# One f32 head product instead of two split ones for the last two batches' group norm, and attention's row maxima spread in two partition parts

## The reference, cut to what matters

```
# layer 0: cross attention to 375 context tokens, 16 heads of 32
a = layernorm(ctx) ; Q, K, V = x Wq, a Wk, a Wv
attn = softmax(Q K^T / sqrt(32)) ; x = x + tanh(gate) * (attn V) Wo
# layer 1: RWKV block, 32 heads of 16
xk, xw, xv, xr, xg = mixes of ln1(x) and its token shift
s = k v^T + w * s ; out = r (u * k v^T + s)            # over the 112 tokens
m  = out.mean(over the 16 of a head)
va = ((out - m) ** 2).mean(over the 16 of a head)
og = (out - m) / sqrt(va + 1e-5) * gn_w + gn_b          # group norm by head
x1 = x + (og * silu(xg Wg)) Wo
xc = ln2(x1) ; result = x1 + sigmoid(..xc.. Wfr) * (relu(..xc.. Wfk)^2 Wfv)
```

## Time and profile before

| | |
|---|---|
| median of 3 runs | 1399.43 us (1397.38 to 1405.21) |
| the profiled execution, its own time | 1399.84 us |
| its span from first to last instruction | 1398.0 us |
| mean granted TensorE clock | 0.979 |
| busy shares | PE 94%, DVE 67%, ACT 54%, POOL 38% |
| `least_cols` | 32 transfers of 437.5 KB |
| `ctx_tok` | 16 pairs of transfers, 672.0 KB (112 partitions) and 78.0 KB (13 partitions) |

### The profile page before, as it was taken

How to read it: one execution, slowest core, us unless ns; L and a number is a source line. 1 busy time by engine, 2 the same in 40 slices (tenths; PEclk the granted TensorE clock), 3 DMA queues, 4 the chain that set the end, 5 groups by cost and what they waited for, 6 DMA issues and landing times.

```text
span 1398.0 us, 42906 instructions
## 1 busy us (share of the span) xinstructions
PE 1319.0 (94%) x17120; PEld 936.5 (67%) x17120; DVE 939.5 (67%) x2416; ACT 752.2 (54%) x1804; POOL 528.5 (38%) x582
## 2 busy tenths in 40 slices
PE   6999999999999999897899999999999999999967
PEld 5777777777777777666666666766676666667624
DVE  3555555555555555547578888888888789887852
ACT  4776677676676677532434453445444544454342
POOL 2221112222222222113547545654566355644550
PEclk9999999999999999987899999999999999999978
DMA  7333322222222222213000010010100010000000
GB/s 228 100 105 107 98 63 69 75 71 70 65 76 76 76 69 92 63 50 136 15 14 22 22 28 14 23 27 21 24 14 26 21 28 11 25 21 21 8 15 14
DMA packets 39402, 73.48 MB, mean 53 GB/s; under 512 B 17781, under 2 KB 20469, under 8 KB 37701
## 3 DMA queue, kind: packets, MB, share of 16 engines
q1 hardware_dynamic: 39237, 71.01, 17.2%
HBM read 60.01 MB, written 7.57 MB: 48 GB/s over the span
## 4 chain that ended last, share of the span: by engine, by line
PE 73%; DVE 13%; issue 8%; ACT 2%; DMA 2%; POOL 1%; SPq 1%; DVEq 0%; POOLq 0%; ACTq 0%
PE b_bank L2017 15%; PE b_bank L2023 12%; PE ring_bank L703 7%; PE ring_bank L704 6%; PE ring_bank L705 6%; PE av_bank L789 4%; PE score_banks L762 4%; DVE probs L450 3%; PE b_bank L2132 3%; PE score_banks L749 3%; PE b_bank L2158 2%; DVE bv L1404 2%; DVE probsT L467 2%; PE av_bank L775 2%; DVE ktil L1398 1%
## 5 line engine op out<-in xcount | busy, mean ns | idle before, releaser
L1139 POOL TENSOR_TENSOR rst<-rp,st 128x448 f32<-128x448 f32 x192 | 202.5, 1078 | 34.9 <-DVE st L1425 32.0
L450 DVE CUSTOM_DVE_ANT_0 probs<-score_banks,unmask 112x375 f32<-112x375 f32 x256 | 124.9, 545 | 93.0 <-issue 93.0
L595 ACT ACTIVATE probs<-probs,least_inv 112x375 f32<-112x375 f32 x256 | 152.7, 609 | 32.5 <-DVE least_inv L450 32.5
L467 DVE SCALAR_TENSOR_TENSOR probsT<-score_banks,least_cols 125x448 f32<-125x448 f32 x192 | 108.0, 618 | 54.2 <-PE score_banks L762 51.8
L610 ACT ACTIVATE probsT<-probsT,key_mask 125x448 f32<-125x448 f32 x192 | 114.7, 662 | 47.6 <-DVE probsT L467 47.4
L1131 POOL TENSOR_TENSOR xm<-mixed,xa 128x448 f32<-128x448 f32 x80 | 89.6, 1129 | 96.1 <-DVE mixed L1354 90.7
L375 POOL TENSOR_TENSOR ctx_rstd<-ctx_var_eps,a_eps_exp 125x3 f32<-125x3 f32 x16 | 13.9, 866 | 272.7 <-DVE ctx_var_eps L423 272.7
L340 POOL TENSOR_TENSOR aT_lo<-whole,aT_hi 128x375 fp32r<-128x375 f32 x64 | 59.0, 922 | 152.3 <-ACT whole L576 150.2
L703 PE MATMUL ring_bank<-aT_hi,wk_lo 128*128 128x376 f32 x256 | 91.2, 356 | 0.9 <-issue 0.9
L1159 POOL TENSOR_TENSOR cen_r<-wkv,sq_r 128x448 fp32r<-128x448 f32 x15 | 17.1, 1140 | 196.6 <-ACT sq_r L1829 196.6
L1354 DVE SCALAR_TENSOR_TENSOR mixed<-b_bank,vec_sb,sx 128x112 f32<-128x112 f32 x320 | 82.5, 324 | 5.6 <-POOL xm L1131 3.9
(11 more groups left out here) (197 smaller groups left out, 3156.6 us busy)
## 6 DMA issues: line engine op xcount, KB each, us to landing
least_cols<-values_of_two_batches SPq DMA_DIRECT2D x32, 437.5 KB
ctx_tok<-in_ctx SPq DMA_DIRECT2D x16, 672.0 KB
xT_sb<-in_xT SPq DMA_DIRECT2D x16, 224.0 KB, 3.0
inv_cols<-values_of_two_batches SPq DMA_DIRECT2D x128, 28.0 KB, 3.7
x_tok<-in_x SPq DMA_DIRECT2D x16, 224.0 KB, 2.7
x_between_layers<-x_tok SPq DMA_DIRECT2D x16, 224.0 KB, 4.6
b_x<-x_between_layers SPq DMA_DIRECT2D x16, 224.0 KB, 2.6
out_dram<-ln_tok SPq DMA_DIRECT2D x16, 224.0 KB, 2.3
```

Source lines behind the costliest of these rows:

```text
L450: dve.tensor_tensor_reduce(out=probs[:, g % 2, i], in0=score_bank[0:T, i, 0:TC], in1=unmask[:, m[1]], scale=-SCALE, scalar=-LOWEST, op0=AL ...
L467: dve.scalar_tensor_tensor(out=probsT[:, g % 2, k].rearrange("p (i t) -> p i t", t=T), in0=score_bank[0:TK, :, k * T:(k + 1) * T], scalar= ...
L595: act.activation(probs[:, g % 2, i], probs[:, g % 2, i], ACT.Exp, scale=-1.0, bias=least_at(m, g, i), accum_out=sums[:, g, i:i + 1]).then_ ...
L1139: pool.tensor_tensor(by_chunk(rst[:, j % NPROD]), by_chunk(rp[:].rearrange("p c t -> p (c t)")), state_of(j), ALU.mult).then_inc(s_pprod, 1)
```

## The change

**Attention.** `spread_rows` reads the maxima back in two transfers, to partitions 0 to 111 and 112 to 124, in place of one to 125. The semaphore that DVE waits on now gets 32 instead of 16 per spread. This is done for all 16 batches.

**Group norm.** For batches 14 and 15 (`in_last_step`) the split is gone. `gn_centre` is one matmul call on `wkv` itself and `gn_var` one on the square, with the matrices read as f32. `norm_high`, `norm_low`, `square_high` and `square_low` are not called for these two batches. PE waits for `wkv_sum` directly and later for `square` directly; the waits that guarded the buffers moved to `square` and `gn_centre`. The 14 batches before keep the split.

```diff
-            sp.dma_start(least_cols[:, 2 * half:2 * half + 2],
-                         rows_in_dram(half, 0).rearrange("(o g) f -> o g f", o=1).broadcast_to([TK, 2, HG * T])).then_inc(s_least_in[half], 16)
+            for part in CTX_PARTS:
+                sp.dma_start(least_cols[part, 2 * half:2 * half + 2],
+                             rows_in_dram(half, 0).rearrange("(o g) f -> o g f", o=1).broadcast_to(
+                                 [part.stop - part.start, 2, HG * T])).then_inc(s_least_in[half], 16)
...
-                dve.wait_ge(s_least_in[g // 2], 16 * count(m, 1, 1))
+                dve.wait_ge(s_least_in[g // 2], 32 * count(m, 1, 1))
...
+    def in_last_step(l):
+
+        return isinstance(l[0], int) and index(l) >= B - 2
...
         def last_steps():                          # gpsimd
             rec_key(m)
-            norm_low(l)
-            square_low(l)
...
             rstd2(l)
-            norm_low(m)
-            square_low(m)
             gate_output(m, False)
...
         def square(l):                             # scalar
             act.wait_ge(s_cen, count(l, 1, 1))
             if is_last(l):
                 act.wait_ge(s_rmm, count(l, 1, 1))
+            elif in_last_step(l):
                 act.wait_ge(s_gated, count(later(l, -1), 1, 1))
...
-            pe.wait_ge(s_gnlo, count(l, 2, 1))     # gn_centre
+            pe.wait_ge(*((s_wkv, count(l, 1, 1)) if in_last_step(l) else (s_gnlo, count(l, 2, 1))))
             if is_last(l):
+                pe.wait_ge(s_gmm, count(l, 1, 1))
...
+            if in_last_step(l):
+                pe.matmul(norm_bank(l)[0][:, 0:CT], centring[:].bitcast(F32), wkv[:].rearrange("p c t -> p (c t)"), start=True,
+                          stop=True).then_inc(s_cen, 1)
+                return
...
-            pe.wait_ge(s_gnlo, count(l, 2, 2))     # gn_var
+            pe.wait_ge(*((s_sq, count(l, 1, 1)) if in_last_step(l) else (s_gnlo, count(l, 2, 2))))
...
+            if in_last_step(l):
+                pe.matmul(norm_bank(l)[1][:, 0:CT], mean_r[:].bitcast(F32), norm_home(l)[1].rearrange("p c t -> p (c t)"), start=True,
+                          stop=True).then_inc(s_var, 1)
+                return
```

More of the change, by code:

```diff
@@ L1152, in norm_low @@
             pool.wait_ge(s_gnhi, count(l, 2, 1))
-            if is_last(l):
-                pool.wait_ge(s_gmm, count(l, 1, 1))
-            elif at_least(l, 1):
+            if at_least(l, 1):
                 pool.wait_ge(s_gaff, count(later(l, -1), 1, 1))
@@ L1824, in norm_high @@
             act.wait_ge(s_wkv, count(l, 1, 1))
-            if is_last(l):
-                act.wait_ge(s_rmm, count(l, 1, 1))
-            elif at_least(l, 1):
+            if at_least(l, 1):
                 act.wait_ge(s_gated, count(later(l, -1), 1, 1))
@@ L1832, in square @@
             act.wait_ge(s_cen, count(l, 1, 1))
+            if is_last(l):
+                act.wait_ge(s_rmm, count(l, 1, 1))
+            elif in_last_step(l):
+                act.wait_ge(s_gated, count(later(l, -1), 1, 1))
             flat = "p c t -> p (c t)"
@@ L1879, in last_steps @@
             chunk_keys_decayed(m)
-            norm_high(l)
             copy_keys(m)
@@ L1886, in last_steps @@
             square(l)
-            square_high(l)
             gn_rstd(l)
             gn_affine(l)
-            norm_high(m)
             square(m)
-            square_high(m)
             xc_affine(l)
```

## The result

Over 14 runs each the changed kernel took 1394.60 us (median, 1390.20 to 1399.38) and the kernel before 1399.74 us (1395.47 to 1405.21): a ratio of 0.9964, 95% interval 0.9948 to 0.9980. That is 5.1 us; the interval leaves 1 out, and the size is under the 0.5% of the prediction's middle case. The predicted 1394.8 lies 0.2 us from the median; the interval allows a gain of 2.8 to 7.3 us, so that a hit this close is luck. The profiled execution took 1396.23 us (span 1394.4, mean clock 0.983), 3.6 us less than the profiled one of before.

A forecast was written before the change was run, and what follows sets the result against it. PE, busy 94% of the span, was taken as the bound, with DMA waits at the seam and waits and clock in the tail. Gains of 2.96 + 0.63 + 1.22 = 4.81 us gave 1394.8 us, 8-in-10 range 1390.8 to 1398.6.

The forecast's parts named there:

- middle case: Whole kernel: measured difference within about 0.5%, 7.0 us, of none; chance 0.75.
- The landing of `least_cols`: At the seam: two parts use more DMA engines and land 3.0 us after issue instead of 6.10.
- Rival 1: At the seam: the two parts land no sooner, 2.96 us not gained, 1398.4 us; chance 0.12.
- The seam, 2.96 us: DVE starts scores 1.47 us earlier, and PE's clock staying up behind the shorter idle time gives 1.49 us.
- both terms pass on: Behind the seam: all later work waits for this chain, so wait and clock gains pass on, 2.96 us.
- Batch 14's group norm, 0.63 us: Tail: PE no longer waits for POOL's second subtraction; DVE is late next, so normalisation, gate and `project_out` come 0.63 us earlier.
- Batch 15's, 1.22 us: Tail: ACT's cast and the split ahead of centring go, 1.83 us, less the f32 call's extra time at low clock.
- the other end: Batch 15's group norm with the clock up: gain of about 2.2 us.
- The sum: Whole kernel: 2.96 + 0.63 + 1.22 = 4.81 us gained, clock turns in the tail put at zero.
- Rival 2: Tail: the clock stays up under batch 14's `project_out`, 8.0 us gained in all, 1391.8 us; chance 0.17.
- Rival 3: Tail: low clock from batch 15's centring lasts through the dense products, 10.4 us lost, 1405.4 us; chance 0.04.
- Rival 4: Seam as forecast, but the tail's 1.85 us taken back by a low-clock `wfk` stretch, 1396.6 us; chance 0.17.

The follow-up runs named there:

- parts of 62 and 63: Changed kernel with the maxima spread in parts of 62 and 63 partitions instead of 112 and 13: 1399.75 us, ratio 1.0003 to the kernel before.
- one transfer of 128: Changed kernel with one maxima transfer over 128 partitions instead of two over 112 and 13: 1395.43 us, ratio 0.9975 to the kernel before.
- group norm alone: Kernel before with only the group norm edit (f32 head products of the last two batches, no splits): 1397.65 us, ratio 0.9993.
- attention part alone: Kernel before with only the attention edit (maxima spread in two parts): 1397.38 us, ratio 0.9989.
- tail filled: Changed kernel with 14 unread matmuls of 128 x 256 in front of TensorE's waits in the last step: 1390.31 us, ratio 0.9939.
- last spread only in parts: Changed kernel with two parts only in the very last maxima spread, the other 31 in one transfer: 1392.83 us, ratio 0.9951.
- fillers in both kernels: Unread matmuls at TensorE's long waits (seam, early steps, last step): kernel before 1389.22 us, changed kernel 1384.26 us.
- everything filled and f32 for all batches: Changed kernel with unread matmuls at TensorE's long waits and f32 head products in all 16 batches: 1377.80 us, ratio 0.9851.

## Why the prediction was right

**The landing of `least_cols`.** The reason (5 of 16 engines) was right, and parts of 62 and 63 and one of 128 show it. The share was 0.81 from 1 to 2 us behind the issue, near the 0.9 forecast. The landing of 3.0 us was too hopeful as far as is known: the transfer of 128 over 16 engines takes a median of 3.7 us, and it shares the queues with the four `inv_cols` behind it; for the two parts no row gives a landing. It cost nothing, since DVE comes 4.3 us after the issue and waits for nobody. Rival 1, a landing no sooner, is excluded.

**The seam, 2.96 us.** Measured 3.12: the wait 1.57, the clock 1.56. That 0.82 us of idle time would leave the clock up was right in every kernel with the faster landing (nine traces, idle time 0.82 to 0.90 us, S 14.78 to 14.87).

**That both terms pass on to the end** is not shown. At the first chunk sums the gain is still there (39.70 us from the third key-major scores before, 36.45 after), though the way from the `wk` product to them scatters: 20.3 to 21.8 us in the traces without fillers behind the seam. Further on it shrinks. From the third key-major scores to the chunk sums at the head of the loop, in traces without fillers in between:

| kernel | us |
|---|---|
| before | 178.00 |
| group norm alone | 178.50 |
| attention part alone | 175.43 |
| one transfer of 128 | 176.68 |
| tail filled | 177.48 |
| last spread only in parts | 177.72 |
| changed | 178.66 |

The last five have the whole gain of the seam and are on average 1.1 us faster than the first two, not 3.1; the best is 2.8 us faster, the changed kernel's own trace 0.4 us slower. Over the 140 us behind the first chunk sums the granted clock was 0.96 in the best of them and 0.91 in the changed kernel, where it was 0.94 in both of the slower landing; in the other three it was 0.94 as well, and what takes their part back is open. (With f32 products in all batches it is 174.99 us, but there these steps are changed too.) With fillers in both kernels the gain passes on: 173.32 us before and 171.55 with the change, for 1.36 of S. The medians can't tell whether 3.1 or 1.1 us arrive: the attention part alone gained 1.5 us, with an interval from 0.8 us slower to 3.9 us faster.

**Batch 14's group norm, 0.63 us.** Measured 0.59. The variance starts 4.45 instead of 6.11 us behind the chunk sums, 1.66 us sooner, and DVE, named as next late, takes all but 0.6 of it.

**Batch 15's, 1.22 us.** Measured 1.18 in the traces where the clock is low there, and 1.90 with fillers in both kernels, where I had put 1.83 + 0.12 plus faster transposes, about 2.2, as the other end. The f32 centring took 1.86 us at the low clock, 0.14 more than the bound of 1.72.

**The sum** of 4.81 us stands against 3.12 + 0.59 + 1.18 = 4.89 by the legs and 5.1 by medians. The three terms are measured each at its place, and to 0.2 us. That their sum is also the difference of the medians rests in part on luck: the interval leaves 2.2 us to either side, and the other legs, put at zero, were +1.22, +2.76, -1.25 and -1.37 us in the one profiled pair, each as large as a term of the sum. Rival 2 (clock up under `project_out(l)`) did not come true as a rule, but it occurs: that product took 3.69 us in two of the seven kernels with f32 products and an unfilled tail (group norm alone, one of 128) and 5.4 to 6.7 in the other five. Where it occurred, the way from the last chunk sums to the `wfk` of batch 15 is 47.06 us; 51.93 less the 1.77 of the two legs would be 50.16, so it is worth 3.1 us, and I had 3.2. In the profiled changed kernel (48.97) some 1.2 us of it are there. Whether the edit made it likelier is open. Rival 3 did not occur. Rival 4's `wfk` stretch did not get longer (4.95 us, and 4.89 before); its time of 1396.6 alone would lie inside the interval.

What I had not asked is where the clock is low though no edit touches it. It was the larger gain: fillers brought the ratio from 0.9964 to 0.9891, some 10 us, in another set of runs; the change brought 5.1.

## What to carry to other kernels

When a transfer that is waited for shows a low DMA share while it is alone, look at its number of partitions: 125 gave 0.34 and 62 gave 0.13, while 112 with a rest of 13, or padding to 128, gave over 0.8. Where TensorE waits ahead of dense products and the clock is low behind it (behind 2.00 and 2.39 us it was here, behind 0.82 it was not), unread matmuls in the gap are worth trying: they cost idle time and bring back what the low clock takes. A gain read at one place should be followed to a later one, since the clock may take it back in between. And before an instruction is priced on a busy engine, look for the one wait per iteration behind it that may swallow the price.

## What was not expected

Much of the scatter of the runs goes with the clock. The kernel before ran from 1392.49 to 1405.32 us over 35 runs, at a mean clock of 0.975 to 0.985 (the correlation of the two is -0.69, which is half of the scatter); the kernel with everything filled and f32 for all batches ran from 1377.32 to 1378.91 over 4, at a mean clock of 0.999 to 1.000. With the clock at its upper level (2.4 GHz) almost throughout, four runs lay within 0.12%; with the unfilled kernels a term of this size is only seen in traces cut into legs. Filled kernels also showed that a filler can itself fall into the low level: ahead of batch 14's output product twelve instructions took 4.41 us where they take 2.86 at the high one, and the product began 1.4 us later than without them, though it then took 3.60 instead of 6.15.
